# Transformer block kernel: projections in three float32r products, the first group's row maxima moved among the last token tiles, and the tokens' selection counts moved into the attention loop

## The reference, cut to what matters

```python
# x: (4, 1024, 256) float32;  16 heads of 16;  16 experts, top 4, in 4 groups of which 2 are allowed; 2 shared experts
xn = layernorm(x)
qkv = xn @ W_qkv + b_qkv                    # 256 -> 768
q, k = rope(q), rope(k)
attn = softmax(q @ k.T / 4) @ v             # per batch and head, 1024 keys
x + attn @ W_out + b_out + moe(xn)          # moe: sigmoid(xn @ w_gate.T), grouped top-4, swiglu experts, shared experts
```

## Time and profile before

| what | value |
|---|---|
| median of three runs | 1217.91 us |
| the profiled execution's span | 1217.1 us |
| PE busy | 1150.2 us (95%) |
| DVE busy | 959.9 us (79%) |
| ACT busy | 750.6 us (62%) |
| POOL busy | 578.9 us (48%) |
| stage A, by the trace | 0 to 158.7 us |
| joint | 158.7 to 198.4 us |
| attention loop, 256 quads | 198.4 to about 844 us |

### The profile page before, as it was taken

The page is one execution under the profiler, slowest core; times in us unless marked ns, Lnnn a source line. Parts: engine busy times, 40 slices in busy tenths (PEclk is TensorE's granted clock), DMA queues, the critical chain, the costliest instruction groups (busy, mean ns, idle before and its releaser), DMA issues. The chain is left out here.

```text
span 1217.1 us, 27786 instructions
## 1 busy us (share of the span) xinstructions
PE 1150.2 (95%) x8310; PEld 582.5 (48%) x8311; DVE 959.9 (79%) x1451; ACT 750.6 (62%) x1568; POOL 578.9 (48%) x861
## 2 busy tenths in 40 slices
PE   4999767999999999999999999998999999998998
PEld 2555422333333333333333333333788887875665
DVE  6575685999999999999999999970555555556888
ACT  3666303888888888888888888887333333330000
POOL 6999947354465653232322323231576666661000
PEclk9999955999999999999999999999999999999999
DMA  6466743454435453343324332402777666655765
GB/s 221 156 202 216 224 110 140 180 163 125 126 106 145 125 143 86 87 109 96 94 80 117 89 95 79 103 29 64 215 225 228 205 204 213 194 165 185 234 220 173
DMA packets 127288, 181.74 MB, mean 149 GB/s; under 512 B 41441, under 2 KB 88929, under 8 KB 125282
## 3 DMA queue, kind: packets, MB, share of 16 engines
q1 hardware_dynamic: 111842, 138.55, 39.6%
q0 software_dynamic: 15360, 42.04, 10.0%
HBM read 99.71 MB, written 80.81 MB: 148 GB/s over the span
## 5 line engine op out<-in xcount | busy, mean ns | idle before, releaser
L1048 DVE TENSOR_REDUCE mx<-pm 128x1 f32<-128x1024 f32 x512 | 620.6, 1222 | 31.4 <-PE pm L1098 30.6
L1022 ACT ACTIVATE pr<-pst 128x512 f32<-128x512 f32 x1024 | 556.6, 596 | 86.3 <-PE pst L1109 34.9
L1098 PE MATMUL pm<-kt,qt 48*128 48x512 f32 x1024 | 386.6, 461 | 13.4 <-DMA qt<-s_q 8.0
L1109 PE MATMUL pst<-qt,kt 50*128 50x512 f32 x1024 | 377.7, 449 | 6.5 <-DMA qt<-s_m 6.5
L1121 PE MATMUL po<-pr,vt 128*17 128x256 f32 x4096 | 322.9, 388 | 9.9 <-ACT osb L1032 9.6
L1098 PEld LDWEIGHTS pm<-kt,qt 48*128 48x128 f32 x1024 | 157.1, 192 | 237.5 <-DVE mx L1048 173.1
L1274 POOL DMA_INDIRECT s_y<-ys_c,slot_c x144 | 139.6, 969 | 85.7 <-issue 46.4
L1121 PEld LDWEIGHTS po<-pr,vt 128*17 128x17 f32 x4096 | 69.0, 95 | 198.9 <-issue 110.3
L1109 PEld LDWEIGHTS pst<-qt,kt 50*128 50x128 f32 x1024 | 152.8, 186 | 18.8 <-ACT pr L1022 10.9
L950 POOL DMA_INDIRECT s_xg<-p_rows,p_slot x128 | 125.2, 978 | 56.0 <-issue 29.8
L1354 PE MATMUL pd<-w13s,xt_c 128*128 x576 | 149.5, 382 | 0.4 <-ACT xt_c L1284 0.4
(11 more groups left out here) (188 smaller groups left out, 1169.5 us busy)
## 6 DMA issues: line engine op xcount, KB each, us to landing
xg<-s_xg SPq DMA_DIRECT2D x144, 128.5 KB
yg<-s_y SPq DMA_DIRECT2D x32, 512.0 KB, 3.9
s_q<-stg SPq DMA_DIRECT2D x32, 256.0 KB
s_k<-stg SPq DMA_DIRECT2D x32, 256.0 KB
kt<-s_k SPq DMA_DIRECT2D x32, 256.0 KB
qt<-s_q SPq DMA_DIRECT2D x64, 128.0 KB
s_o<-osb SPq DMA_DIRECT2D x32, 256.0 KB, 6.9
w13s<-w SPq DMA_DIRECT2D x1, 4608.0 KB, 14.6
```

The source lines that it names most:

```text
L1022: nc.scalar.activation(pr[:, (k % 2) * 4 + ORDER[i], :], pst[bank(gg, k, i)][:, :], ACT.Exp, scale=SCALE).then_inc(exp_ok, 1)
L1048: nc.vector.tensor_reduce(mx[:, half, col:col + 1], pm[slot][:, :, :].rearrange("p a n -> p (a n)"), AX.X, ALU.max).then_inc(mx_free, 1)
L1098: mm = pe.matmul(pm[slot][:, kk, :], qt[buf][rows, half, pair, qi * P:(qi + 1) * P], kt[buf][rows, pair, kk * 512:(kk + 1) * 512], start=T ...
L1109: pe.matmul(pst[bank(buf, k, i)][:, :], kt[buf][rows, pair, kc * P:(kc + 1) * P], qt[buf][rows, half, pair, :], start=True, stop=True)\
```

## The change

It has four parts.

1. Stage A's projections use float32r. ACT makes `wh`, the weights' high part, and POOL `wl`, the rest, once; for each tile ACT makes `xh` beside `xt`, and DVE makes `xl = xt - xh`. Each float32 product becomes three float32r ones.
2. All 32 uses of group 0 are done in stage A, two a step in steps 22 to 37 (`EARLY`), with one `pm` buffer. `pT` and `pV` have one buffer instead of two to make room. SP loads group 0's keys and queries from step 15 on, and the half 0 rows are split, turned and stored at step 31.
3. Nothing of PE's work is left in the joint (`FILL` is 0). The routing of the last batch moves from stage A's end to DVE's first work of stage B; `choose` follows it on POOL. The two counting matmuls stand in quad 13 of group 0, in the place of its maxima, which follow after ACT's two copies. POOL's planning and the loads of the experts' weights come two half groups and two groups later.
4. Stage A's loops are written out, and two more rounds of stage B's on DVE and SP; buffers are shared (`work`, `sg_d`, `qt1` as the fourth `xT`).

```diff
@@ stage A, POOL
+                if buf == 0:
+                    pool.wait_ge(const_ok, 7)
+                    pool.wait_ge(w_in, 17)
+                    nc.gpsimd.tensor_tensor(wl[:], wsb[:], wh[:].bitcast(F32), ALU.subtract).then_inc(w_in, 1)
+                    pool.wait_ge(w_in, 18)
@@ stage A, DVE
+            def low(k, t, b):
+                dve.wait_ge(xt_ok, k + 1)
+                v.tensor_tensor(xl[:, t % 2, :, :], xt[:, t, :, :], xh[:, t % 2, :, :].bitcast(F32), ALU.subtract)\
+                    .then_inc(xl_ok, 1)
-            steps(dve, B, TPB, NT, [(0, other_stats), (BACK, rest), (TPB, routing)])
+            for n in range(NT + BACK):
+                t, b = n % TPB, n // TPB
+                if n < NT:
+                    other_stats(n, t, b)
+                if 0 <= n - PROJ < NT:
+                    low(n - PROJ, (n - PROJ) % TPB, (n - PROJ) // TPB)
+                early(n, 0)
+                if n >= BACK:
+                    rest(n - BACK, (n - BACK) % TPB, (n - BACK) // TPB)
+                early(n, 1)
+                early(n, 2)
+                if TPB <= n < NT:
+                    routing(n - TPB, t, b - 1)
+                if n == TURN_A:
+                    turn_rows(nc, dve, first, 0, 0, 0)
@@ stage A, ACT
+            act.wait_ge(w_in, 16)
+            nc.scalar.activation(wh[:], wsb[:], ACT.Copy).then_inc(w_in, 1)
+                nc.scalar.activation(xh[:, t % 2, :, :], pT[:, 0:C].rearrange("p (c n) -> p c n", c=CC),
@@ stage A, PE
             def project(k, t, b):
-                pe.wait_ge(xt_ok, k + 1)
+                pe.wait_ge(xl_ok, k + 1)
                 for c in range(CC):
-                    mm = pe.matmul(pQ[t % 2][:, :], xt[:, t, c, :], wsb[:, c, 0:2 * C],
-                                   start=False, stop=(c == CC - 1))
+                    for n, (a, w) in enumerate(splits):
+                        mm = pe.matmul(pQ[t % 2][:, :], a[:, t % 2, c, :], w[:, c, 0:2 * C],
+                                       start=False, stop=(c == CC - 1 and n == 2))
+def early_use(n, spot):
+
+    if spot >= EARLY.get(n, 0):
+        return None
+    return sum(count for at, count in EARLY.items() if at < n) + spot
+FIRST_LOADS = 15
+FILL = 0
+EARLY = {n: 2 for n in range(22, 38)}
+SPLIT_A, TURN_A, ROWS_A = 31, 31, 31
@@ stage B, DVE, ahead of the loop
-            for use in range(AHEAD):
-                if use == FIRST_ROWS:
-                    turn_rows(0, 0, 0)
-                maximum(use, use % 2, use)
+            nc.vector.memset(po[:, :], 0.0).then_inc(po_ok, 1)
+            for piece in range(5):
+                route(nc, dve, routed, first["gb"], keep, B - 1, piece, first["ex_ok"], first["ex_used"], keep["passed_dve"])
@@ stage B, PE, in quad COUNT = 13 of group 0
+            def counts(freed):
+                pe.wait_ge(sel_ok, 1)
+                need(pe, mx_free, freed)
+                pe.matmul(pm[0][:, 0, :], keep["ones"][:], sel, start=True, stop=True)
+                pe.matmul(pm[0][:, 1, :], keep["below"][:], sel, start=True, stop=True).then_inc(pre_ok, 1)
+                        if counting:
+                            pe.wait_ge(keep_ok, 2)
```

More of the change, by code:

```diff
@@ L98, in rounds, with rounds_last @@
         emit(j)
-def rounds_last(eng, n, emit):
-    emit(0)
-    with eng.Fori(1, n - 1) as j:
+def rounds_last(eng, n, emit, head):
+    for j in range(head):
+        emit(j)
+    with eng.Fori(head, n - 1) as j:
         emit(j)
@@ L135, in straight, with stage_a @@
                 part(k, k % per, k // per)
-def stage_a(nc, x, w_qkvg, b_qkv, rope, s_q, s_k, s_v, s_xn, s_xt, keep, first):
+def stage_a(nc, x, w_qkvg, b_qkv, rope, s_q, s_k, s_v, s_xn, s_xt, s_m, keep, first):
     W = 3 * C + E
@@ L292, in sines @@
                 nc.gpsimd.tensor_tensor(qr[:, sl, :], rc[:, sl, :], rs[:, sl, :], ALU.add).then_inc(qr_ok, 1)
-            steps(pool, B, TPB, NT, [(PROJ, sines)])
+            for n in range(NT + PROJ):
+                if n >= PROJ:
+                    sines(n - PROJ, (n - PROJ) % TPB, (n - PROJ) // TPB)
+                if n == SPLIT_A:
+                    pool.wait_ge(mx_free, 16)
+                    split_maxima(nc, own, first, 0, mp_ok)
         @block.vector
@@ L340, in _ @@
             setup = own.n
+            first["setup"] = setup
             def other_stats(k, t, b):
-                if not isinstance(k, int):
+                if b:
                     return
@@ L840, in rows @@
             def rows(n, half, buf):
[L842 to L849 removed]
+                store_rows(sp, s_m, first, n, half)
+                load_rows_back(sp, s_m, first, n, half, buf)
             def store(u, half, j, gg):
@@ L882, in body @@
                     rows(2 * g + 1, 1, gg)
+                    if isinstance(g, int) and g == 0:
+                        load_v(1, 0, 1)
                     if isinstance(g, int) and g < 2:
-                        weights(g)
+                        store_half(sp, s_q, s_k, first["stg"], B - 1, g, first["st_out"][g])
+                    if isinstance(g, int) and 2 <= g < 4:
+                        weights(g - 2)
                     if not (isinstance(g, int) and g >= NG - 2):
@@ L1003, in body @@
                             send(*tile)
-            for j in range(3):
+            for j in range(4):
                 body(j)
-            with pool.Fori(3, NG // 2 - 1) as j:
+            with pool.Fori(4, NG // 2 - 1) as j:
                 body(j)
@@ L1018, in body @@
                         q = g * QUADS + k
+                        if isinstance(g, int) and g == 0 and k == COUNT:
+                            act.wait_ge(pre_ok, 1)
+                            for kk, (name, done) in enumerate((("tiles", keep_ok), ("pre", keep_ok))):
+                                nc.scalar.activation(keep[name][:].rearrange("p n e -> p (n e)"), pm[0][:, kk, :], ACT.Copy)\
+                                    .then_inc(done, 1)
                         need(act, pv_ok, 2 * (q - 1))
```

375 lines of the change are left out of this document (214 added, 161 removed).

## The result

The changed kernel takes 1277.72 us (median of 4 runs, 1263.1 to 1283.7) against 1217.82 us for the kernel before in the same comparison: a ratio of 1.0467, 95% interval 1.0405 to 1.0529. Its profiled execution has a span of 1274.3 us. It is slower, as predicted, but by 60 us and not by 6.

| kernel | loop starts | loop | rest | span |
|---|---|---|---|---|
| before | 198.4 | 644.1 | 374.6 | 1217.1 |
| changed | 226.9 | 672.4 | 375.0 | 1274.3 |

The account below looks back on a forecast made before the run. It took POOL to bound stage A, DVE the joint, two DVE maxima a quad the loop. Loop start +2.1, low clock 0, counts +3.9: +6.0 on 1217.1, with 0.8 around it 1223.9, said as 1224, range 1206 to 1237.

Parts of the forecast that it names:

- Start of stage A: Before the first projection, wl and xl of tile 0 come first: POOL starts at 28.0 instead of 21.72, taken as +6.5 us.
- xl at 0.9 us: In stage A, each tile's xl operation on DVE beside POOL takes 0.9 us, bounds 0.43 and 1.7.
- Steps up to 21: In stage A POOL still sets the pace: +1 us from xl, +1 from routing lag, DVE 4 us behind at step 22.
- Steps 22 to 37: In late stage A DVE sets the pace: 78.7 us of work plus bubbles and a wait, 87 us, bounds 72 and 92.
- Clock in late steps: Seven late steps with routing pieces leave PE idle and may lower its clock: 4 us over all, bounds 0 and 15.
- low clock for good: Rival: PE stays at the low clock in the late steps; half of them lost gives +13, 1237 us; chance 0.11.
- Low clock at the loop's start: The loop starts at the low clock as before, costing the same 6.3 us: no change, bounds 0 and 12.
- Counts: In the loop's quad 13, the counting matmuls and ACT's copies delay DVE's next maximum: 3.9 us, bounds 1.5 and 5.
- Moved loads, planning, weights: In the loop, these stay hidden at 0.39 DMA share: 0, at worst 2 us for group 1's rows.
- Exposed weight loads: Rival: float32r products do not overlap their weight loads, making PE the bound from tile 0: +35, 1253 us; chance 0.04.
- Cheap late steps: Rival: DVE and POOL rarely meet, late steps take 74 us instead of 87; half gives 1207 us; chance 0.30.
- the joint's whole length: Rival: late steps fit under POOL's 4.04 us, so 30 us go, 1190 us; given no chance of its own.

Follow-up runs that it names:

- a1: The kernel before with only its projections split into float32r products (wh, wl, xh, xl), joint and all else as before; 1245.2 us, ratio 1.0225.
- d4: The changed kernel with xl made one step earlier on DVE's queue, behind stg and ahead of the routing piece; 1243.3 us, ratio 1.0223.
- a3: The changed kernel with six spare products of 512 columns ahead of PE's wait for xl in steps 22 and later; 1264.7 us, ratio 1.0409.
- b1: a1 with xl made one step earlier on DVE's queue, behind stg and ahead of the routing piece; ratio 1.0113.
- a2: The changed kernel with its projections plain as before, keeping the 32 early maxima and all that moved with them; 1234.2 us, ratio 1.0135.
- c2: The same kernel as d4, run on a chip where the kernel before takes about 1390 us; ratio 1.0035.
- b2: a2 with the counts copied by DVE instead of ACT, and the weights w13 loaded in group 1 instead of group 2; ratio 1.0154.

## Why the prediction was wrong

Two steps failed. Before the loop, the steps with routing and the late ones were taken to go at DVE's pace with `xl` and routing as work to be added up; they go at the pace of a chain of waits in which `xl` stands behind routing. In the loop, the moved counts, planning and loads were priced at 3.9 us and nothing; with the falls of the clock behind their pauses they cost some 27.

- *Start of stage A, +6.5.* Right: first rope at 27.94 (28.0), by the steps given.
- *xl at 0.9 us, bounds 0.43 and 1.7.* Right enough: 0.76 on average in the changed kernel.
- *Steps up to 21: "The first batch's lag of 5 us goes in the distance at which PE runs ahead of POOL: +1."* This failed. Tile 18's rope came at 108.81, not 102.0. The lag is not bought back: while DVE is in a routing piece PE cannot start the next projection, so it has no distance left; in a1, without any maximum in these steps, tile 18's rope came at 113.66, later still.
- *Steps 22 to 37: "Now DVE sets the pace", 87 us with 7 of bubbles.* The wrong form, and most of the error before the loop: DVE was busy 86 of 126 us, a step with a routing piece took 7.1 to 10.1 us where 7 was expected, one without 4.8 to 5.2 where 4.5 was. A chain that goes from DVE to PE to ACT to POOL and again through DVE has no bound engine; its length is that of the waits in turn, which I had counted as small corrections. From tile 18's rope to the loop 118.1 us went by; d4 needed 97.3 with the same work, and what the prediction had was 97. The first loads of group 0 in step 15 and 17 had no term; behind them ACT waited 6.3 us, and POOL 5.2 for it.
- *Clock in late steps +4, bounds 0 and 15; low clock for good as a rival, +13.* The clock stood at 0.50 for some 70 of the 126 us, which is near the rival's condition. What it cost there stays open: a3 took 4.2 us off by raising it, less what its own products cost, and b1 and d4 mend waits and clock together (0.81 from 100 us to the loop in d4).
- *Low clock at the loop's start: 0, bounds 0 and 12.* 23.5 us instead of 14.8 (the 14.2 of the earlier trace rows ends 0.6 us early), 3.7 us, in the bounds.
- *Counts, +3.9.* Measured 3.1 as a stall; the term left out is the clock behind it, 10.2 us at 0.50, 4.3 us more. In a2 the same stall had no fall behind it, so this much is a matter of chance.
- *Moved loads, planning, weights: 0, at worst 2.* The second step that failed: 8.3 us of late rows and splits, and the falls behind them, 27.3 us at 0.50, 11.4 us. The DMA share of 0.39 on which I argued is a mean; what matters is that a round trip of 16 KB has 0.5 to 3 us of slack and stands behind what was issued before it. The 2 us allowed for late rows were meant for group 1's rows behind the last batch's stores; the late ones stood behind the weights' loads.
- *Rivals.* Exposed weight loads: wrong, six products follow each other at 0.23 us with the load of each beneath it. Cheap late steps and the joint's whole length: wrong for the changed kernel, though a2 got 3.4 us of it. The direction came out right, but the two terms that carried it, the start and the counts, are 9 of the 57 us, so it was in good part luck.

## What to carry to other kernels

Before pricing an operation that is put into an in-order queue, write down what stands in front of it there and who waits for it: here 0.8 us of work a tile cost 20 to 27 us by its place, and one line moved gave them back. Moving work off a slow stretch moves the transfers and waits that it had hidden; look at each round trip with little slack, and at what is issued ahead of it, not at mean shares. In this kernel's loop, which PE keeps full, a pause of PE of 1.3 to 3.5 us costs itself and in most cases 3 to 20 us at half the clock behind it, by my estimate at 0.42 us each.

## What the runs showed of the hardware

- In the changed kernel's loop the granted clock fell to 0.50 within 1.2 us behind pauses of PE of 1.3 us (271.8), 3.5 (365.3) and 1.6 (412.3), and behind the third it stayed there longest, 20.5 us with PE busy throughout; behind one of 1.6 us at 338.5 it did not fall. In a2 the counts' stall, the same 1.3 us for PE, brought no fall at all. In the ten traces from chips where the kernel before takes 1217 us, 21 of 29 pauses of 1.2 to 3.5 us in the loop were followed by a fall within 2.1 us, 3 to 20.5 us long, 8 were not; the kernel before and a1, without such a pause, had none.
- The kernel before took 1216 and 1218 us (medians) on two chips and 1389 to 1391 on three others, and the ratio of a change was not the same on both kinds: c2 1.0035, d4 (the same kernel) 1.0223, with intervals that do not overlap; by the medians of all executions 1.011 and 1.021.
- A store of 16 KB from SP to DRAM let its load be issued after 1.4 us at rest, after 3.6 and 3.9 us when it stood 17 us behind a load of 4.6 MB, and after 16.8 us when it stood 4 us behind it (b2).
- A float32r product of 512 columns took 0.23 us at the full clock and 0.43 at the low one, of 272 columns 0.13 and 0.23, with no weight load exposed (loads of 0.19 and 0.33 us beneath it).
